# A transformer layer with eight experts on one core: only the routed rows go through the experts

## The reference

```python
x = x + attention(layernorm(x))                  # q and k rotated, causal softmax
h = layernorm(x).reshape(-1, 256)                # 2048 tokens
scores = softmax(h @ gate_w.T)                   # 8 experts
topk_w, topk_idx = top_k(scores, 2); topk_w = topk_w / sum(topk_w)
y_all = einsum(silu(h @ w1[e]) * (h @ w3[e]), w2[e])   # w1, w3: 256x176, w2: 176x256
y = sum over the two chosen experts of topk_w * y_all
x = x + y + (silu(h @ sw1) * (h @ sw3)) @ sw2     # shared part, inner width 352
```

## Time and profile before

| what | us |
|---|---|
| median of three runs (859.29 to 860.8) | 859.47 |
| span of the profiled execution | 858.3 |
| PE busy in it | 833.2 |
| DVE, ACT, POOL busy in it | 669.2, 537.5, 382.2 |
| steady attention, one sequence | 69.8 |
| expert stage, one tile of 128 tokens | 16.2 |

### The profile page before, as it was taken

How to read it: one execution, slowest core, us unless ns; L and a number is a source line. 1 busy time by engine, 2 the same in 40 slices (tenths; PEclk the granted TensorE clock), 3 DMA queues, 4 the chain that set the end, 5 groups by cost and what they waited for, 6 DMA issues and landing times.

```text
span 858.3 us, 18971 instructions
## 1 busy us (share of the span) xinstructions
PE 833.2 (97%) x6272; PEld 804.6 (94%) x6272; DVE 669.2 (78%) x1924; ACT 537.5 (63%) x1676; POOL 382.2 (45%) x339
## 2 busy tenths in 40 slices
PE   4899999999999999999999999998999999999998
PEld 4788999999999999999999999887999999999998
DVE  6898889888888888888988889996565556556554
ACT  4787777777777777777777778887333332332332
POOL 4777556656556665655665656773000000000000
PEclk9999999999999999999999999999999999999999
DMA  7443000000000000000000000330000000000000
GB/s 222 129 137 78 1 1 2 1 0 0 0 0 0 0 0 0 0 0 0 0 0 0 0 0 18 72 105 13 7 6 12 6 6 12 6 6 6 12 6 13
DMA packets 20221, 18.86 MB, mean 22 GB/s; under 512 B 4096, under 2 KB 17120, under 8 KB 20192
## 3 DMA queue, kind: packets, MB, share of 16 engines
q1 hardware_dynamic: 20192, 18.50, 7.3%
HBM read 16.39 MB, written 2.10 MB: 22 GB/s over the span
## 4 chain that ended last, share of the span: by engine, by line
PE 83%; DVE 8%; ACT 3%; POOL 3%; issue 2%; DMA 1%; SPq 0%; DVEq 0%; POOLq 0%
PE bank L381 70%; PE bank L421 4%; PE bank L520 3%; PE bank L414 3%; PE bank L430 3%; DVE work L635 3%; POOL work L344 1%; DVE work L628 1%; DMA stage<-in_L_attn_wq 1%; DVE w_lo L601 1%; ACT w_hi L884 1%; DVE work L644 1%; DVE pt_lo L656 1%; ACT work L901 1%; POOL w_lo L1068 1%
## 5 line engine op out<-in xcount | busy, mean ns | idle before, releaser
L344 POOL TENSOR_TENSOR work<-work 128x512 f32<-128x512 f32 x127 | 165.3, 1301 | 109.9 <-DVE work L635 109.7
L1040 POOL TENSOR_TENSOR qkt_lo<-work,qkt_hi 128x512 fp32r<-128x512 f32 x128 | 165.7, 1295 | 95.9 <-ACT qkt_hi L894 95.9
L635 DVE TENSOR_TENSOR work<-bank,sinn 64x512 f32<-64x512 f32 x256 | 176.2, 688 | 3.4
L381 PE MATMUL bank<-w_hi,xnt_lo 128*128 128x352 f32 (+2 forms) x448 | 160.1, 357 | 1.2 <-DVE work L822 0.8
L381 PE MATMUL bank<-w_lo,xnt_hi 128*128 128x352 f32 (+2 forms) x448 | 154.5, 345 | 0.0
L381 PE MATMUL bank<-w_hi,xnt_hi 128*128 128x352 f32 (+2 forms) x448 | 153.3, 342 | 0.0
L381 PE MATMUL bank<-xnt_hi,w_lo 128*128 128x256 f32 x512 | 146.2, 286 | 3.0 <-POOL w_lo L1068 3.0
L381 PE MATMUL bank<-xnt_lo,w_hi 128*128 128x256 f32 x512 | 146.0, 285 | 0.0
L381 PE MATMUL bank<-xnt_hi,w_hi 128*128 128x256 f32 x512 | 145.9, 285 | 0.0
L951 ACT ACTIVATE work<-bank 128x176 f32<-128x176 f32 x128 | 40.6, 318 | 157.9 <-PE bank L381 157.8
L894 ACT CAST qkt_hi<-work 128x512 fp32r<-128x512 f32 x128 | 79.5, 621 | 83.5 <-POOL work L344 81.4
(11 more groups left out here) (91 smaller groups left out, 2243.7 us busy)
## 6 DMA issues: line engine op xcount, KB each, us to landing
stage<-in_L_ffn_w SPq DMA_DIRECT2D x32, 88.0 KB, 2.0
resid<-in_L_attn_x SPq DMA_DIRECT2D x8, 256.0 KB, 3.8
stage<-in_L_attn_wq SPq DMA_DIRECT2D x8, 256.0 KB, 3.7
stage<-in_L_attn_wk SPq DMA_DIRECT2D x8, 256.0 KB, 3.7
stage<-in_L_attn_wv SPq DMA_DIRECT2D x8, 256.0 KB, 4.1
stage<-in_L_attn_wo SPq DMA_DIRECT2D x8, 256.0 KB, 2.9
out_x<-resid SPq DMA_DIRECT2D x16, 128.0 KB, 1.7
stage<-in_L_ffn_sw SPq DMA_DIRECT2D x4, 176.0 KB, 2.3
```

The source lines that it names most:

```text
L344: eng.tensor_tensor(roped[:, a], rope_cos[:, a], rope_sin[:, a], ALU.add).then_inc(rope_add, 1)
L381: mm = pe.matmul(out, lhs[a], rhs[b], start=start and n == 0, stop=stop and n == 2, skip_group_check=more)
L635: op = nc.vector.tensor_tensor(rope_sin[lo:lo + 64, a], p_qk[a][hi:hi + 64, :, :], sn, ALU.mult)
L1040: nc.gpsimd.tensor_tensor(qkt[a][1][:, :, :], roped[:, a], qkt[a][0][:, :, :], ALU.subtract).then_inc(qkt_lo, 1)
```

## The change

The router no longer runs in the tile loop. For every sequence but the last it runs inside the attention of the next one: DVE normalises the rows a second time into `xn2`, PE transposes them (`turn_rows`), multiplies by the gate (`gate_scores`) and counts, by a product with a triangular matrix, how many rows before this one go to the same expert (`ranks`); DVE and POOL turn this into two row numbers for each token. POOL then writes each normalised row to its two places in a table in DRAM that is ordered by expert (`send`, four indirect DMAs for a sequence), and stores the transposed rows for the shared part (`store_turned`). The table is cleared beforehand by nine DMAs. The PE work of the router uses banks 0 and 1 between the projections. The last sequence's router runs in the shared tiles behind the attention.

Behind the attention come eight shared tiles, then the expert stage: DVE writes a list of 39 tiles, with an expert and a first row for each (each expert's rows rounded up to whole tiles), PE and SP load their entry of the list into a register, SP loads 128 rows, PE multiplies them by that expert's weights at an address computed from the register, and SP stores the result over the rows. Eight more shared tiles follow, beside which POOL fetches each token's two results (32 indirect DMAs), and DVE adds them with their weights (`finish`).

Also changed: five staging slots for six; `roped` now lies on the cosines' product; the second and third matmul of `three` are exchanged; five DMAs of constants are added behind piece 13. Cut to its core:

```diff
-NSTAGE = 6
+NSTAGE = 5
...
+            def rows_in(t):
+                if t >= XSLOTS:
+                    sp.wait_ge(xs_lo, t - XSLOTS + 1)
+                sp.wait_ge(xt_stored, 16 * (t // ST + 1))
+                src = xt_d[t // ST][:, t % ST * D:(t % ST + 1) * D].rearrange("p (c s) -> p c s", c=DC)
+                sp.dma_start(xs_slot[t % XSLOTS], src).then_inc(xs_in[t % XSLOTS], 16)
+            def clear(k):
+                wait(sp, cleared, 16 * k)
+                rows = slice(k * S, min((k + 1) * S, REGION))
+                here = xs_d[0:E * REGION, :].rearrange("(e r) d -> e r d", e=E)[:, rows, :]
+                zero = zero_t[0:rows.stop - rows.start, :]
+                sp.dma_start(here, zero[None, :, :].to_broadcast([E, rows.stop - rows.start, D])).then_inc(cleared, 16)
...
+                if n == plan["last", 13][0] + NSTAGE:
+                    sp.wait_ge(rope_mul, B * N)
+                    for t in range(ST):
+                        rows_in(t)
...
+                if n == 13:
+                    sp.dma_start(xt2[:, 0:2, :], order_t).then_inc(order_in, 16)
+                    sp.dma_start(route[:, :], route_t).then_inc(route_in, 16)
+                    sp.dma_start(base[:, :], base_t).then_inc(route_in, 16)
+                    with nc.allow_non_contiguous_dma(reason="the router's 2048 weights are transposed"):
+                        for c in range(DC):
+                            sp.dma_start(gate_t[:, c, :], gate_w[:, c * P:(c + 1) * P].rearrange("e p -> p e")).then_inc(
+                                route_in, 16)
...
+                if n == NATT + NSTAGE - 1:
+                    for k in range(B + 1):
+                        clear(k)
+                    sp.wait_ge(cleared, 16 * (B + 1))
+                    sp.dma_start(xs_d[E * REGION:XROWS, :].rearrange("(e r) d -> e r d", e=E),
...
+            def tile_start(j):
+                return nc.values_load(tile_row[0:1, j:j + 1], engines=(mybir.EngineType.SP,), min_val=0,
+                                      max_val=XROWS - P, skip_runtime_bounds_check_because="a tile of the list")
+            def tile_in(j):
+                if j >= XSLOTS:
+                    sp.wait_ge(xe_ps, j - XSLOTS + 1)
+                row = tile_start(j)
+                sp.dma_start(x_slot[j % XSLOTS], xs_d[bass.ds(row, P), :]).then_inc(x_got[j % XSLOTS], 16)
+            def tile_out(j):
+                sp.wait_ge(ye_cp, j + 1)
+                row = tile_start(j)
+                sp.dma_start(xs_d[bass.ds(row, P), :], y_slot[j % XSLOTS]).then_inc(y_out[j % XSLOTS], 16)
...
+            sp.wait_ge(plan_done, 2)
+            for j in range(XSLOTS):
+                tile_in(j)
+            for j in range(NJ):
+                if j + XSLOTS < NJ:
+                    tile_in(j + XSLOTS)
+                tile_out(j)
+                if NJ - 8 <= j < NJ - 8 + XSLOTS:
+                    rows_in(S1 + j - (NJ - 8))
+            for t in range(S1 + XSLOTS, NT):
...
+                for n, (a, b) in enumerate(((1, 0), (0, 0), (0, 1))):
                     mm = pe.matmul(out, lhs[a], rhs[b], start=start and n == 0, stop=stop and n == 2,
...
+                        if b is not FIRST:
+                            if h == 6:
+                                pe.wait_ge(xt2_cp, b)
+                            if h == 7:
+                                pe.wait_ge(logit_done, b)
+                            if h == 10:
+                                pe.wait_ge(place_done, 2 * b)
...
+                    if b is LAST and h >= 14:
+                        up_s(0, h - 14)
...
+                    if b is not FIRST and h in (5, 6, 9):
+                        pe.wait_ge(rope_mul, j0 + h + 4)
+                        if h == 5:
+                            turn_rows(b)
+                        if h == 6:
+                            gate_scores(b)
+                        if h == 9:
+                            ranks(b)
...
+            def turn_rows(n):
+                pe.wait_ge(xn2_done, n)
+                for t in range(ST):
+                    for c in range(DC):
+                        mm = pe.transpose(p_turn[:, t * DC + c, :], xn2[:, t, c * P:(c + 1) * P], ident[:, :])
+                mm.then_inc(xt2_ps, 1)
+            def gate_scores(n):
+                pe.wait_ge(xt2_cp, n)
+                for t in range(ST):
+                    for c in range(DC):
+                        mm = pe.matmul(p_gate[:, t, :], xt2[:, t * DC + c, :], gate_t[:, c, :], start=c == 0, stop=c == DC - 1)
+                mm.then_inc(gate_ps, 1)
+            def ranks(n):
+                pe.wait_ge(routed, (n - 1) * RP + 4)
+                first, second = member[:, 0:E], member[:, E:ST * E]
+                pe.matmul(p_rank, order[:, 0, :], member[:, :], start=True, stop=False)
+                pe.matmul(p_rank[:, E:ST * E], order[:, 1, :], first, start=False, stop=True)
+                pe.matmul(p_total, order[:, 1, :], first, start=True, stop=False)
+                pe.matmul(p_total, order[:, 1, :], second, start=False, stop=True).then_inc(rank_ps, 1)
...
+            def turn_x(j):
...
+                pe.wait_ge(x_got[j % XSLOTS], 16 * (j // XSLOTS + 1))
...
+            def up_e(j, e):
+                pe.wait_ge(xe_lo, j + 1)
+                if j >= 2:
+                    pe.wait_ge(acts_e_done, j - 1)
+                for c in range(DC):
+                    mm = three(p_ue[j % 2][:, 0:UW], [xe_t[b][:, j % 2, c, :] for b in range(2)],
+                               [ups[b][:, bass.ds(e + 2, 1), c, :] for b in range(2)], c == 0, c == DC - 1)
+                mm.then_inc(ue_ps, 1)
...
+                for k, r in ((0, P), (1, E_TAIL)):
+                    mm = three(p_yy[j % 2], [act_e[b][0:r, j % 2, k, :] for b in range(2)],
+                               [downs_e[b][0:r, bass.ds(e, 1), k, :] for b in range(2)], k == 0, k == 1)
...
+            def tile_expert(j):
+                return nc.values_load(tile_e[0:1, j:j + 1], engines=(mybir.EngineType.PE,), min_val=0,
+                                      max_val=E - 1, skip_runtime_bounds_check_because="an expert of the list")
...
-            def tile_step(t):
-                more = t is not LAST_TILE
-                for u in range(3, NU):
-                    if u >= 4:
-                        pe.wait_ge(act_done, t * NR + read_by(u - 4))
-                    up(u)
...
+            for t in range(1, S1):
+                for u in range(2):
+                    up_s(t, u)
+                if t == 2:
+                    turn_rows(B)
+                if t == 3:
+                    gate_scores(B)
+                if t == 5:
+                    ranks(B)
+                turn_s(t - 1)
+                if t > 1:
+                    down_s(t - 2)
...
+            pe.wait_ge(plan_done, 2)
+            e = {}
+            for j in range(2):
+                e[j] = tile_expert(j)
+            turn_x(0)
+            for j in range(NJ):
+                if j + 1 < NJ:
+                    turn_x(j + 1)
+                up_e(j, e[j])
+                if j + 2 < NJ:
+                    e[j + 2] = tile_expert(j + 2)
+                if j >= 1:
+                    turn_e(j - 1)
+                if j >= 2:
+                    down_e(j - 2, e[j - 2])
+            for u in range(2):
+                up_s(S1, u)
...
                         residual(b - 1)
+                    if b is not FIRST:
+                        if h == 1:
+                            rows_stats(b, b - 1)
+                        if h == 2:
+                            rows_mv(b)
+                        if h == 3:
+                            rows_norm(b, b - 1)
+                        if h == 6:
+                            compare(b)
+                        if h == 8:
+                            rows_rank(b)
+                        if h == 9:
+                            places(b)
+                        if h == 12:
+                            reduce_both(b)
...
+            def finish(t):
+                if t < NT:
+                    dve.wait_ge(came[t], 32)
+                    if t >= S1:
+                        dve.wait_ge(ys_add, t + 1)
+                    nc.vector.scalar_tensor_tensor(resid[:, t, :], back[0][:, t, :], wtop[:, 0, t:t + 1], resid[:, t, :],
+                                                   ALU.mult, ALU.add).then_inc(fin_first, 1)
+                if t > 0:
+                    dve.wait_ge(fin_first, t)
+                    nc.vector.scalar_tensor_tensor(resid[:, t - 1, :], back[1][:, t - 1, :], wtop[:, 1, t - 1:t],
+                                                   resid[:, t - 1, :], ALU.mult, ALU.add).then_inc(fin_done, 1)
...
-            def route(tile, meanwhile=lambda: None):
...
-                step(1, nc.vector.tensor_copy(logit[:, :], p_u[0][:, UW:UP]))
-                step(2, nc.vector.max(top[:, :], logit[:, :]))
```

(62 more changed lines are left out.)

794 lines of the change are left out of this document (501 added, 293 removed).

## The result

The changed kernel takes 958.82 us (median of 4 runs, 958.14 to 960.09) against 859.61 in the same session: a ratio of 1.115 (1.114 to 1.117). The forecast was 854, its range ended at 900. The direction and the size are both missed. The profiled span is 958.0, to be set against the 852.7 of the sum: 105.3 us too few.

The account below looks back on a forecast made before the run. PE's instruction count was taken to bound the kernel. Attention ending at 592.8 plus 2.5, 51 and 2 gave 648.3; then 36 to the first expert tile, loop 123, end 45.4: 852.7, plus 1.2 around the span, 854 us; range 800 to 900.

Parts of the forecast that it names:

- Start: Kernel start: fewer staging slots, five more DMAs among the first weights and an ACT wait add 2.5 us (0 to 5).
- Sends: Head 12: POOL issues four indirect DMAs at 1.0 us each, 5.5 us late, 4.0 of it on PE per sequence.
- Gathers more than 1.2 us apart: End of the kernel: gathers further than 1.2 us apart would prove the prediction wrong on the slow side.
- The other routing: Router work inside each attention sequence: PE 1.5 us, POOL waits 0.2 at head 2 and 1.0 at head 6, 0.6 at head 8.
- full reserve: Attention: POOL idles 1.45 us between two heads and may then be 1.5 us late before PE stands.
- The 0.6 at head 8: Attention, head 8: DVE has 0.8 us of ranks before the 1.47 us of the norm, costing about 0.6 us.
- The last sequence: Last attention sequence, where weights are split as well: 2 us more.
- To the first expert tile: After attention: last sequence's routing takes 36 us beside 26 us of shared PE work, so PE stands 10 us.
- The loop: Expert loop: a store, load and landing cycle sets 3.15 us a step, 123 us for 39 steps.
- The end: After the loop: last result's landing, 32 gathers at 1.0 us each, additions and last store take 45.4 us.
- dear sends: Rival: 64 indirect DMAs on the path; gain gone from 1.1 us each, 886 us at 1.5, 899 at 1.7; chance 0.16.
- the 123 us to be had: Expert stage: PE's work falls from 259 us to 136 us, so 123 us could be gained before waits.

Follow-up runs that it names:

- the experiment with the other order: In SP's expert loop, the load for tile j+4 put ahead of the store of tile j-1, against the changed kernel: 908.0 us, 2.46 us a step.
- waits that never hold: Changed kernel with POOL waiting, before the gathers for tile t, for those of tile t-8, which had landed long before: 961.5 us, end 82.9.

## Why the prediction was wrong, by its own steps

The miss is 105.3 us of span. The terms, each as measured less as forecast:

- **Start**, 2.5: it was 5.3 (the first norm of the second sequence at 79.30, before at 74.04), just past its upper bound. With ACT's copy of the order moved it came at 75.89. 2.8 us.
- **Sends**, 4.0 a sequence: the way (POOL late, then ACT, then PE) is right to the instruction. The size is 7.05: 1.27 us a send for 1.0 makes 5.1 of the 5.4 of standing, and the clock's 1.5 was not in the sum at all. Gathers more than 1.2 us apart were the prediction's own sign of being wrong on the slow side. The clock was 1.00 in all of the earlier trace rows, and I did not ask what it does when a new wait of this length appears. 3.05 x 7 = 21.4 us.
- **The other routing**, 3.3 a sequence: 7.0 in the kernel without sends, 2 of PE's own for 1.5, and 4.8 of waits for 1.8. The waits for ACT's L1225 stand at heads 2 and 6 (0.8 and 1.6, with 0.3 behind each for POOL's low part) and were put at 0.2 and 1.0, as if POOL had its full reserve. At head 10 PE waits 1.4 for DVE to add the ranks; the sum had no such term. The 0.6 at head 8 did not show as a wait of PE. 3.73 x 7 = 26.1 us.
- **The last sequence**, 2: PE stood 9.4 us at 697.8, ahead of the first shared tile, whose rows SP could load only once POOL had split the weights, which stood behind the four sends. Queues behind POOL were named for the ordinary sequence and not followed here. What is left of the attention's 58.5 is 8.2 us.
- **To the first expert tile**, 36: 44.2, the sends' 1 us and, by my reading, longer small steps between three engines, which no run takes apart. 8.2 us.
- **The loop**, 3.15 us a step: 3.33. The formula with the measured 0.49 for the register gives (2.3 + 4.3) / 2 = 3.3. The mechanism held and its one guess was 0.15 short, but that the mean agrees is in part luck: the alternating pair takes 6.28 us and not 6.6, and the rest are slow steps one behind the other, which the formula doesn't have. 8.5 us. It was foreseen, and 33 us were lost to the order of two lines, as the experiment with the other order shows.
- **The end**, 45.4: 56 without the stand (32 gathers at 1.27 are 8.6 more, and 2 behind them), 75.5 with it, 30.1 us in all. The 19 us are a thing that no row of before held.

The steps that failed are thus the size of a send and the clock behind its wait, the waits of the other routing and the end. The clock was also 0.88, 0.91 and 0.71 on the way to the first expert tile, in the loop and in the end; it was in none of these terms, and what it costs there is not shown.

The rest of the change cost nothing that shows in a head without routing: PE's transposes come 4.33 us apart there (273.97 and 278.30), as before, with the matmuls in the other order and `roped` on the cosines' product.

Among the rivals, dear sends came nearest. But its formula at 1.27 us, 854 + 64 x 0.27 = 871, is still 88 us off, and no single rival could reach 959: the range added up small errors as if they were one. Seven repetitions turned 3 us here and 3.7 there into 47. Before, 265.5 us lay between 592.8, where the prediction's count has the attention end without its additions, and the end at 858.3. PE's work there is 136 now and takes 251, and the attention ends 114 us later, at 706.8: that is where the 123 us to be had went.

What stays open is the mechanism of the stand. It hangs on something that a shift of code changes, but one and eight instructions leave it, waits that never hold leave it, and what helps one kernel doesn't help the next. The DMA records name packets of two instruction queues. In the seven kernels without the stand one of queue 8 comes 10.9 to 11.6 us behind the first gather and one of queue 14 at 13.3 to 13.4. In all ten with it that of queue 14 comes only at 42.9 to 48.4 us, when the last gather has been issued, and that of queue 8 at 37.9 us or later in eight, at 8.0 and 10.4 in the other two. So the stand goes with a late packet of queue 14 without an exception. Whether the engines stand because their instructions are not loaded, or load none because they stand, is not shown.

## What to carry to other kernels

Work put into a loop that runs seven times must be priced against the engine's time per pass and not against how late it may be once: here POOL's idle time was 1.45 us a head, and its 1.5 us of reserve was gone after one send. Price an indirect DMA by the time that it takes of POOL (1.27 us for one of 128 rows) and look what is queued behind it. A store that stands ahead of the next load in one queue ties the step to the whole round trip; exchanging them was worth 33 us.

## What was not expected of the hardware

- Indirect DMAs of 128 rows go out every 1.27 us (0.96 and 0.30 of issue), plain ones of the same size from the same engine every 0.54.
- PE's clock fell to 0.50 behind a wait of 5.4 us and stayed at 1.00 when matmuls without a purpose filled it; at this place that is worth 1.5 us.
- While POOL issues 32 indirect DMAs, ACT can stand for 13 to 24 us and DVE for another 11 to 15 behind it without a cause in the trace, and PE waits for them, in ten of the seventeen kernels here that issue them. It makes 19 us of the time. In the changed kernel 64 empty instructions at the head of DVE or POOL took it away.
